# Two of a norm's four small GpSimd operations done on VectorE, and the up weights' low parts computed in four places instead of one

## The reference

```python
def _layernorm(x, axis=-1, eps=1e-05):
    m = jnp.mean(x, axis=axis, keepdims=True)
    v = jnp.var(x, axis=axis, keepdims=True)
    return (x - m) / jnp.sqrt(v + eps)
...
    h = _layernorm(x, axis=-1) * (1 + ca) + sa
    x = x + ga * _L0_attn_ref(h, ...)          # mix, k/v/r projections, scan over t, Wo
    h = _layernorm(x, axis=-1) * (1 + cb) + sb
    x = x + gb * _L0_ffn_ref(h, ...)           # router top 2 of 8, silu(g) * u, down
...
    g = jnp.einsum('nh,ehm->enm', x, Wg)
    u = jnp.einsum('nh,ehm->enm', x, Wu)
    eo = jnp.einsum('enm,emh->enh', jax.nn.silu(g) * u, Wd)
```

## Time and profile before

| | |
|---|---|
| median of 3 runs | 374.97 us (373.86 to 377.30) |
| the profiled execution | 377.31 us |
| its span in the trace | 375.50 us |
| busy share of the span | PE 94%, DVE 83%, ACT 71%, POOL 12% |

### The profile page before, as it was taken

The page is one execution under the profiler, slowest core; times in us unless marked ns, Lnnn a source line. Parts: engine busy times, 40 slices in busy tenths (PEclk is TensorE's granted clock), DMA queues, the critical chain, the costliest instruction groups (busy, mean ns, idle before and its releaser), DMA issues.

```text
span 375.5 us, 4537 instructions
## 1 busy us (share of the span) xinstructions
PE 352.0 (94%) x1447; PEld 249.4 (66%) x1447; DVE 313.5 (83%) x617; ACT 267.9 (71%) x439; POOL 46.4 (12%) x75
## 2 busy tenths in 40 slices
PE   4895986899999999999999999999999999989986
PEld 1462543667867776766867677677776686868765
DVE  5987997899999899999889999999799979752541
ACT  3897896958896499849996899759994996141210
POOL 4300063000400230001400140011300100010000
PEclk9997897799999999999999999999999999999999
DMA  8931020000003000500030004000100001000001
GB/s 273 276 111 44 2 98 0 2 1 0 0 3 112 0 3 0 154 2 1 1 114 0 0 2 130 25 0 2 41 16 3 0 0 58 0 0 33 26 0 56
DMA packets 16240, 14.86 MB, mean 40 GB/s; under 512 B 4767, under 2 KB 15193, under 8 KB 16217
## 3 DMA queue, kind: packets, MB, share of 16 engines
q1 hardware_dynamic: 16184, 14.58, 12.8%
q10 hardware_dynamic: 32, 0.01, 0.0%
HBM read 10.38 MB, written 4.21 MB: 39 GB/s over the span
## 4 chain that ended last, share of the span: by engine, by line
PE 84%; ACT 5%; DVE 5%; issue 2%; POOL 2%; DMA 1%; SPq 0%; ACTq 0%; DVEq 0%; POOLq 0%
PE mm L998 31%; PE yo L1029 19%; PE mm L929 18%; PE yo L950 6%; PE tp L849 3%; PE cb L1010 1%; POOL n_rstd L355 1%; PE cb L961 1%; PE cb L963 1%; PE cb L849 1%; DVE n_stats L1306 1%; DMA pool_x<-in_L_wmod_dram 1%; PE mm L1049 1%; PE cb L981 1%; ACT n_xn L380 1%
## 5 line engine op out<-in xcount | busy, mean ns | idle before, releaser
L929 PE MATMUL mm<-mixed,WT 128*128 128x512 f32 x192 | 91.1, 611 | 3.7 <-DVE mixed L1321 3.7
L1029 PE MATMUL yo<-WdG,act 128*128 128x256 f32 x320 | 71.8, 380 | 1.6 <-DVE act L1523 1.6
L1029 PEld LDWEIGHTS yo<-WdG,act 128*128 128x128 f32 x320 | 59.6, 190 | 10.2 <-DVE act L1523 2.7
L929 PEld LDWEIGHTS mm<-mixed,WT 128*128 128x128 f32 x192 | 36.9, 196 | 39.2 <-issue 31.8
L998 PE MATMUL mm<-h_h,w_up_h 128*128 128x512 f32 x160 | 53.5, 416 | 0.0
L998 PE MATMUL mm<-h_l,w_up_h 128*128 128x512 f32 x160 | 50.8, 399 | 0.0
L998 PE MATMUL mm<-h_h,w_up_l 128*128 128x512 f32 x160 | 50.6, 398 | 0.0
L352 POOL TENSOR_TENSOR n_ve<-n_mv,small 128x4 f32<-128x4 f32 x16 | 7.3, 458 | 281.4 <-DVE n_mv L1310 281.4
L511 ACT ACTIVATE pool_g<-mm 128x512 f32<-128x512 f32 x40 | 23.5, 588 | 22.4 <-PE mm L998 22.4
L998 PEld LDWEIGHTS mm<-h_l,w_up_h 128*128 128x128 f32 x160 | 30.5, 191 | 7.5
L998 PEld LDWEIGHTS mm<-h_h,w_up_l 128*128 128x128 f32 x160 | 30.3, 190 | 7.5
(11 more groups left out here) (163 smaller groups left out, 570.0 us busy)
## 6 DMA issues: line engine op xcount, KB each, us to landing
x_in<-in_L_attn_x_dram SPq DMA_DIRECT2D x8, 512.0 KB, 5.0
out_dram<-pool_x SPq DMA_DIRECT2D x5, 512.0 KB, 3.2
gate_rows<-gate_dram SPq DMA_DIRECT2D x4, 384.0 KB, 4.6
pool_x<-in_L_wmod_dram SPq DMA_DIRECT2D x2, 512.0 KB, 6.1
out_dram<-x_third SPq DMA_DIRECT2D x2, 512.0 KB, 3.3
pool_x<-in_L_wmod_dram SPq DMA_DIRECT2D x2, 256.0 KB, 3.9
pool_g<-in_L_ffn_Wg_dram SPq DMA_DIRECT2D x2, 256.0 KB, 5.0
pool_g<-in_L_ffn_Wu_dram SPq DMA_DIRECT2D x2, 256.0 KB, 4.4
```

The source lines that it names most:

```text
L929: last = nc.tensor.matmul(mm[PROJECT_BANK[c.n][j]][:, :], WT[:, w, kc, oc * P:(oc + 1) * P], mixed[:, w, kc, :], start=(kc == 0), stop=(kc ...
L1029: last = nc.tensor.matmul(dst, act[:, e, t * P:(t + 1) * P], WdG[:, e, :], start=(e == 0), stop=(e == NB - 1))
```

## The change

VectorE, right behind a norm's `BN_AGGR`, waits for `mv_done`, adds eps (`n_ve`) and multiplies the mean by -1 (`n_mr`); for norm1 of c0, whose shift nobody needs, only the first. GpSimd then does two operations: the power, and `n_shift` = `n_mr` * `n_rstd`. `low_up()`, four subtractions in a row, becomes four calls `low_up(gu, kc)` between other work of VectorE; the first `up` waits for the two gate parts and the second for all four. TensorE gets one more `fill` before `turn1(c2, 0)`.

```diff
@@ class Norm
+                self.ve_done = sem(f"{name}_ve_done")
@@ gpsimd rstd
-                step = 3 * c.n - (2 if norm is norm1 and c.n else 0)
-                wait(pool, norm.mv_done, TT * (c.n + 1))
+                step = c.n - (1 if norm is norm1 and c.n else 0)
+                wait(pool, norm.ve_done, 2 * c.n + (2 if norm is norm2 else 1))
                 wait(pool, norm.xn_done, TT * c.n)
-                nc.gpsimd.tensor_tensor(norm.ve[:, :], norm.mv[:, :, 1], small[:, 0, :], ALU.add
-                                        ).then_inc(norm.pool_step, 1)
-                pool.wait_ge(norm.pool_step, step + 1)
                 nc.gpsimd.tensor_tensor(norm.rstd[:, :], norm.ve[:, :], small[:, 1, :], ALU.pow
                                         ).then_inc(norm.rstd_done if direct else norm.pool_step, 1)
                 if direct:
                     return
-                pool.wait_ge(norm.pool_step, step + 2)
-                nc.gpsimd.tensor_tensor(norm.mr[:, :], norm.mv[:, :, 0], norm.rstd[:, :], ALU.mult
-                                        ).then_inc(norm.pool_step, 1)
-                pool.wait_ge(norm.pool_step, step + 3)
-                nc.gpsimd.tensor_tensor(norm.shift[:, :], small[:, 2, :], norm.mr[:, :], ALU.subtract
+                pool.wait_ge(norm.pool_step, step + 1)
+                nc.gpsimd.tensor_tensor(norm.shift[:, :], norm.mr[:, :], norm.rstd[:, :], ALU.mult
                                         ).then_inc(norm.rstd_done, 1)
@@ tensor up
                 if i == 0:
                     pe.wait_ge(h2lo_done, c.n + 1)
-                    if c.n == 0:
-                        pe.wait_ge(up_lo_done, 4)
+
+                if c.n == 0 and i < 2:
+                    pe.wait_ge(up_lo_done, KH * (i + 1))
@@ tensor order
             project(c1, (4, 5))
+            fill(yo[1], 1)
             turn1(c2, 0)
@@ vector stats
+                ve.wait_ge(norm.mv_done, TT * (c.n + 1))
+                nc.vector.tensor_scalar(norm.ve[:, :], norm.mv[:, :, 1], EPS, None, ALU.add).then_inc(norm.ve_done, 1)
+                if norm is norm2 or c.n:
+                    nc.vector.tensor_scalar(norm.mr[:, :], norm.mv[:, :, 0], -1.0, None, ALU.mult
+                                            ).then_inc(norm.ve_done, 1)
@@ vector low_up
-            def low_up():
-                for kc in range(KH):
-                    for gu in range(2):
+            def low_up(gu, kc):
@@ vector order
             mix(c1, 2)
-            low_up()
+            low_up(0, 0)
             scan_weight(c1, 1)
+            low_up(0, 1)
             low_part(c0)
+            low_up(1, 0)
             offset(c1, 0)
+            low_up(1, 1)
             bias_in(c1)
```

More of the change, by code:

```diff
@@ L1553, in stats2 @@
                 stats(norm2, x1[c.n % 3], c, (x1_done, 2 * (c.n + 1)))
-            def low_up():
-                for kc in range(KH):
-                    for gu in range(2):
[L1558 to L1561, removed]
+            def low_up(gu, kc):
+                ve.wait_ge(up_hi_done, 2 * kc + gu + 1)
+                nc.vector.tensor_tensor(w_up_l[:, kc, gu, :], w_up[:, kc, gu, :],
+                                        w_up_h[:, kc, gu, :].bitcast(F32), ALU.subtract).then_inc(up_lo_done, 1)
             def normalise_direct():
```

## The result

On one chip, in 20 runs each, the kernel before took a median of 376.31 us and the changed kernel 374.25 us. The ratio is 0.9956, with a 95% interval from 0.9938 to 0.9974, so the change gains 1.7 us (1.0 to 2.3), or 0.4%. The quotient of the two medians is not that ratio: it is 0.9945, or 2.1 us, which lies in the same interval. The forecast was 2.3 us off a median of 374.97, the median of three runs. Of the 1.55 us by which 372.7 misses, 1.34 are that starting point.

The account below looks back on a forecast made before the run. TensorE bounds the middle; time can be won where it waits, at norm1 of c2. -2.8 + 0.27 + 0.2 = -2.3 us, taken from the 374.97 us median, gave 372.7 us; range 370.0 to 376.0.

Parts of the forecast that it names:

- Part 1, GpSimd: At norm1 of c2 the power gets in between the mix's halves, `n_shift` ends near 56.2 us, `route(c0)` 2.4 us earlier.
- The rival of a late GpSimd: At norm1 of c2 the power is held until `low_part` ends and nothing is won: 1.0 us slower, 376.0 us; chance 0.12.
- Part 1, `down(c0, 0)`: `down(c0, 0)` starts 2.8 us earlier, set by VectorE; TensorE waits about 1 us there and loses its remaining gain.
- The rival in which TensorE keeps its gain: Up to `down(c0, 0)` VectorE binds less than thought, so 4.9 us are gained: 370.1 us; chance 0.2.
- Part 2, the cost of the added operations: 31 added VectorE operations in 16 norms cost 0.27 us at the start, 0.2 at the end, 0 in the middle.
- The start: `stats1(c1)` stands ahead of `mix(c0, 0)`, for which TensorE waits: +0.27 us, fully on the path.
- The end: The last `weigh` and `spread_comb` have no slack, so TensorE's delay goes through: +0.2 us.
- The middle: Slack of 0.5 us ahead of `spread_comb` takes the added operations: 0, with 3.2 us as the upper bound.
- the rival without slack: In the middle each `stats2` and `stats1` from c1 on puts 0.27 us on TensorE: 375.9 us; chance 0.08.
- Norm2 of c0: The power waits for one scan's end and `n_shift` for the next, at 52.15 us against 52.17: no gain.
- GpSimd locks VectorE out in turn: At norm1 of c2 VectorE stands still for the power and `n_shift`; gain falls to 1.1 us, 373.9 us; chance 0.05.
- I expect the full clock to stay: At norm1 of c2 TensorE's idle time falls from 3.5 to 0.2 us, so its clock stays at 1.00.

Follow-up runs that it names:

- norm_only: The changed kernel with the four subtractions in one block again, `up` waiting for all four, and no added filler: 373.44 us, ratio 0.9932 to the kernel before.
- split_only: The kernel before with only the four subtractions spread and the split wait of `up`, its norm unchanged, no added filler: 374.35 us, ratio 0.9939.
- dve_more: The changed kernel with one needless 128x1024 VectorE addition (1.13 us) behind `down_weight(c0)`: 375.69 us, ratio 0.9979 to the kernel before.
- before_again: The kernel before, unchanged, run once more for another trace: 373.96 us.
- placed: The changed kernel with norm1(c1)'s added VectorE operations moved behind `mix(c0, 0)`, norm2(c7)'s behind the next `weigh`: 374.12 us, ratio 0.9946 to the kernel before.
- low_on_gpsimd: The changed kernel with `low_up(1, 0)` and `low_up(1, 1)` on GpSimd instead of VectorE: 374.36 us, ratio 0.9954 to the kernel before.
- fill_only: The kernel before with only four filler calls (3.4 us) added ahead of `turn1(c2, 0)`: 375.54 us, ratio 0.9972.
- split_warm: The kernel before with subtractions spread, plus four filler calls each ahead of `turn1(c1, 1)` and `project(c1, (0, 1))`: 374.49 us, ratio 0.9965.
- split_mid: As split_warm, with one more filler call in the middle of `modulate_rest`: 375.20 us, ratio 0.9974 to the kernel before.

## Why the prediction missed, and what of it held

The replay of norm1 of c2 came out, and so did the prices of the added operations. What went wrong is how the sum was put on a median, and which part of it was the clock's.

**Part 1, GpSimd.** Right. The power was issued ahead of the first half of the mix and got in between the halves, as `n_ve` had; `n_shift` ended 12.78 us behind the scan (55.68 - 42.90), where 56.2 - 43.53 = 12.67 was forecast. `n_xn` came 2.47 us earlier against the scan (2.28 forecast), TensorE's wait of 3.5 us is gone, and `route(c0)` is 2.67 us earlier (21.43 us behind the scan, was 24.10; 2.4 forecast). The rival of a late GpSimd falls, even with half the change missing: norm_only and split_only each show one GpSimd operation held again (2.72 and 2.13 us), and it still lands in time or 0.7 us late. My working took both halves together and didn't ask whether one would do; one does.

**Part 1, `down(c0, 0)`.** Right in the trace: 2.90 us for 2.8, a wait of TensorE of 1.02 us for VectorE where I said about 1. dve_more shows that a delay of VectorE arrives there. The rival in which TensorE keeps its gain falls.

**The step that failed** is the sentence "The runs' median is 2.3 us lower than that execution, so I forecast 374.97 - 2.3". It goes wrong twice. Its base is the median of three executions, 374.97 us, where 20 gave 376.31: that is 1.34 us of the 1.55 missed. And it takes the whole of a gain that was read from one execution off a median of executions that partly don't have it. Of the 2.90 us, 1.80 (51.45 - 49.65) are the half clock from 61 to 71 us, which the kernel before has in some executions only; 1.10 us (49.65 - 48.55) are GpSimd's delay and the order, and those are there at full clock as well. Against an execution with the fall the net is -2.90 + 0.33 (end) + 0.25 (start) = -2.3, the forecast; against one without it -1.10 + 0.58 = -0.5. With 38 of 96 executions of the first kind the sum is -0.4 x 2.3 - 0.6 x 0.5 = -1.2 us. Measured were 1.7 (1.0 to 2.3), and the mean spans of 96 and 32 executions differ by 374.36 - 372.68 = 1.7. (The medians of the 20 give 2.1.) The half microsecond or more that is left over is not explained: the executions of clock 0.99 and more also differ by 0.95 us between the two kernels (373.4 and 372.45), not by 0.5. The start, which varies by 4 us in itself, may hide it; no run shows that.

With 376.31 as its base the same step would have given 374.0, 0.2 us from the measured median. By this account that would have been luck, since only 38 of 96 executions have a gain of 2.3 us to give.

The clock is also where the sum had a wrong cause. VectorE's waits of 0.85 (inside its 2.4), 0.35 and 0.31 us were taken as what a norm in time gives back; in before_again the norm is as late and they are gone already. The prediction gave the half clock 1.6 us of TensorE's surplus, lost to VectorE, and said that it "would eat TensorE's surplus, not VectorE's gain". In the kernel before it cost the stretch up to `down(c0, 0)` 1.80 us. Whether it would in the changed kernel no run shows, since the clock never fell there.

The hint was there: the median lay 2.3 us below the profiled execution, and one trace says nothing of the clock in the other two.

**Part 2, the cost of the added operations.** The start: 0.27 forecast; the mix starts 0.56 us behind the first aggregate (12.62 and 13.18) and 0.30 before, so 0.26. (The four terms of the forecast add up to 0.29. The 0.05 for the semaphore stood in no row; at norm1 of c2 `n_ve` now starts 0.04 us behind the end of the aggregates, 53.29.) The wait ahead of the first projection, 1.42 to 1.61 us in eight traces without them and 1.51 to 2.02 in six with them, is 0.26 longer in the mean, too. The end: 0.2 forecast, 0.33 measured, and `placed` takes it back. The middle: 0, as forecast (117.51 and 117.49 us), since TensorE has 41.00 us of work in 41.00; the rival without slack falls. The stretch: 0.55 us between split_only and the changed kernel, for three norms, where 3 x 0.27 would be 0.8. Norm2 of c0: 0, as forecast, though not as told: `n_shift` came 1.0 us earlier against the scan and didn't wait for the next scan's end, but ScalarE took it up only 0.07 us earlier (51.50 - 42.90 = 8.60 us behind the scan, was 8.67).

**GpSimd locks VectorE out in turn.** Not at norm1 of c2: the mix took 1.41 us with the power in it (1.38 without), the scan 1.27. For wide operations it does, as low_on_gpsimd shows.

**The clock.** "I expect the full clock to stay" held at 61 to 71 us in every trace of the changed kernel. What I took for the cause of the fall, the wait of 3.5 us, doesn't force one: before and before_again have the same wait, one at 0.50 and the other at 1.00 behind it. The other twelve traces, with a wait of at most 1.44 us there, are all at 1.00.

## What to carry to other kernels

Before a gain that rests on a granted clock is subtracted from a median, see whether the clock is the same in other executions: split the saving into the part that is there at full clock and the part that isn't, and weigh the second by how often it happens. A small GpSimd operation that is in the way can be helped from either side, by fewer operations on GpSimd or by breaking up the row of two-input VectorE operations; take the side that adds nothing to an engine that binds later. Moving elementwise work of two SBUF inputs onto an idle GpSimd is not free while VectorE does the same.

## What the runs showed of the hardware

GpSimd doesn't get in at every change of VectorE's instructions. A waiting GpSimd operation passed over the change from mix to subtraction (before, before_again, split_only, fill_only) and from subtraction to subtraction (4.33 and 2.72 us); it got in from the first half of a mix to the second, from a subtraction to a scan, and behind `low_part` or a subtraction where VectorE was idle next. What the skipped ones have in common is that the next instruction is a `w_up_l` subtraction; why that should matter stays open.

The power held VectorE up by nothing that is visible (1.41 and 1.38 us for the mix), while beside a GpSimd subtraction of 128x640 VectorE's took 2.10 us instead of 0.80.

TensorE's clock also fell with no idle time of TensorE ahead of it: in split_warm it counts as busy from 17 us on, with 32 matmuls of 4 columns from 20.60 to 24.23 us, and the clock is 0.50 from 25 to 28 us. The same matmuls stand ahead of full clock in split_only. What starts that fall was not found; with the fillers of split_warm and split_mid it is still in both traces.
